# A graph kernel on one core: node rows moved as 112 and 13 partitions, the opening reordered, the second table by fifths in six banks

## The reference, cut to what matters

```
h = relu(layernorm(x)); x = x + L0(h)     # message layer: the part that the change touches most
   L0: m = relu(h[src] @ W_msg[:256] + h[dst] @ W_msg[256:] + b_msg)
       agg = segment_sum(m, dst); out = layernorm(relu([h, agg] @ W_upd + b_upd)) * gamma + beta
h = ...; x = x + L1(h)     # sums, maxima and means of edge attributes by node, then an MLP
h = ...; x = x + L2(h)     # attention over the edges
h = ...; x = x + L3(h)     # feat @ W_self + max over edges of (relu(feat @ W_pool))[src] * weight, @ W_neigh
```

## Time and profile before

| | |
|---|---|
| median of 3 runs | 2512.22 us (2509.89 to 2512.85) |
| profiled execution | 2510.97 us, span 2508.7 us |
| PE / DVE / ACT / GpSimd busy | 1118.0 / 1420.4 / 455.4 / 1437.0 us |
| share of the span | 45 / 57 / 18 / 57 % |
| DMA | 447.51 MB, mean 178 GB/s |

### The profile page before, as it was taken

One profiled execution on the slowest core, in us unless ns is written; L12 is line 12 of the kernel. 1 busy time (PEld: TensorE's weight loads), 2 busy tenths in 40 slices (PEclk: granted clock), 3 DMA queues, 4 the chain that ended last, 5 costly groups with the idle time before them and its releaser, 6 DMA issues. The chain is left out here.

```text
span 2508.7 us, 19387 instructions
## 1 busy us (share of the span) xinstructions
PE 1118.0 (45%) x4862; PEld 802.8 (32%) x4862; DVE 1420.4 (57%) x3644; ACT 455.4 (18%) x952; POOL 1437.0 (57%) x1447
## 2 busy tenths in 40 slices
PE   5597778787557249999930000000024111111105
PEld 4486667666334135556620000000013000000004
DVE  4397777676999932222236666666665444434342
ACT  3022222221011101111110000000014333333331
POOL 2577777776246040010057777777743777777774
PEclk9799999999766559999965555555557555555557
DMA  4697777775887720000036666666643666666663
GB/s 126 195 285 237 240 230 228 236 234 152 279 265 253 248 62 3 13 14 9 9 93 209 209 209 208 209 208 209 208 133 119 206 213 208 211 211 209 211 208 127
DMA packets 204961, 447.51 MB, mean 178 GB/s; under 512 B 38899, under 2 KB 114564, under 8 KB 204850
## 3 DMA queue, kind: packets, MB, share of 16 engines
q1 hardware_dynamic: 136107, 263.40, 29.4%
q0 software_dynamic: 67936, 182.02, 27.1%
q10 hardware_dynamic: 806, 0.87, 0.1%
HBM read 276.43 MB, written 169.68 MB: 178 GB/s over the span
## 5 line engine op out<-in xcount | busy, mean ns | idle before, releaser
L390 POOL DMA_INDIRECT msg_rows<-message_source_table,source x416 | 402.8, 968 | 193.7 <-issue 178.6
L1733 POOL DMA_INDIRECT att_rows<-att_table,lane_source x416 | 419.8, 1009 | 126.8 <-issue 126.8
L1754 POOL DMA_INDIRECT att_rows<-message_source_table,lane_source x416 | 393.5, 946 | 158.2 <-issue 126.4
L492 PE MATMUL msg_ps_sum<-msg_by_edge,msg_rows 128*128 128x128 f32 x1664 | 225.3, 293 | 97.7 <-DVE aggT L603 96.0
L492 PEld LDWEIGHTS msg_ps_sum<-msg_by_edge,msg_rows 128*128 128x128 f32 x1664 | 210.9, 204 | 129.3 <-issue 128.3
L1837 PE MATMUL late_ps<-ident,att_largest 128*4 128x128 f32 x1 | 0.4, 374 | 551.6 <-DVE att_largest L1963 551.6
L1885 PE MATMUL late_ps<-w_selfT,hT 128*125 128x256 f32 x100 | 49.7, 649 | 403.6 <-DVE x L2122 403.6
L480 PE MATMUL msg_ps_window<-msg_window,msg_by_node 128*128 128x256 f32 x832 | 206.4, 394 | 21.3 <-issue 21.3
L1309 POOL DMA_INDIRECT att_terms<-aggT,first_edge x25 | 29.5, 1180 | 323.9 <-ACT aggT L1433 323.9
L2115 DVE SCALAR_TENSOR_TENSOR att_rows<-att_rows,lane_line,late_ps_share 128x256 f32<-128x256 f32 x208 | 99.9, 480 | 173.8 <-ACT late_ps_share L1817 164.6
L1985 DVE SCALAR_TENSOR_TENSOR aggT<-aggT,lane_carry,att_rows 128x260 f32<-128x260 f32 x388 | 190.3, 490 | 13.6
(11 more groups left out here) (320 smaller groups left out, 2265.5 us busy)
## 6 DMA issues: line engine op xcount, KB each, us to landing
att_states<-aggT SPq DMA_DIRECT2D x104, 528.0 KB
msg_window<-message_window_table SPq DMA_DIRECT2D x416, 128.0 KB
best_states<-att_rows SPq DMA_DIRECT2D x104, 512.0 KB
attr_states<-attr_work SPq DMA_DIRECT2D x26, 768.0 KB
attr_states<-aggT SPq DMA_DIRECT2D x26, 768.0 KB
attr_work<-in_edge_attr SPq DMA_DIRECT2D x36, 384.0 KB
msg_line<-place_line SPq DMA_DIRECT2D x52, 256.0 KB
msg_rows<-message_source_table,source POOLq DMA_INDIRECT x416, 3.7
```

The costliest lines, as they stand in the source:

```text
L390: nc.gpsimd.indirect_dma_start(rows[:, s, t, :], None, self.source_table, bass.IndirectOffsetOnAxis(ap=self.source[:, at:at + 1], axis=0)) ...
L492: last = nc.tensor.matmul(ps_sum[s % 2][:, t, k, :], rows[:, s, t, k * P:(k + 1) * P], by_edge[:, s % BUFS, t, :], start=True, stop=True)
L1733: nc.gpsimd.indirect_dma_start(rows[:, t % ring, :], None, self.attention_table, bass.IndirectOffsetOnAxis(ap=self.lane_source[:, t:t + 1] ...
L1754: nc.gpsimd.indirect_dma_start(best_rows[:, g % SLOTS, t, :], None, self.source_table, bass.IndirectOffsetOnAxis(ap=self.lane_source[:, g ...
```

## The change

Six things change, the arithmetic of the outputs stays the same but for the broadcast of places by PE.

1. Every load or store of 125 partitions on SP's queue becomes two, of 112 and 13 partitions (`SHARES`): `x`, both tables, the attention table, the last source table and the output.
2. DVE makes the first fifth's statistics first; those of the next fifth come in two pieces behind the copies of the first and second block of a fifth, the aggregation behind the second, the reciprocal behind the fourth. ACT goes block by block, rows two blocks ahead of the copy. PE waits for the weights only before the first product.
3. The lists of first nodes are loaded from ACT's queue, behind all copies; the window loads wait for them.
4. Source stores are counted by fifths. The bias is added to a fifth as soon as that fifth's source rows are out. The products of the second table have six banks instead of two.
5. The places are no longer stored and spread by the DMA. PE spreads them (`spread_places`): a column of the identity in bf16, repeated 128 times, times `rel16`, into the first bank of the group's own `ps_window`; DVE compares from there. `rel16` stays in SBUF.
6. In the loop, PE's order becomes `gather_sums` 1, `spread_places` 5, `expand` 4; the wait for `added` moves from `expand` to `spread_places`. On DVE `add` and `by_nodes` change places.

```diff
+EVEN = NT // 16 * 16
+SHARES = (slice(0, EVEN), slice(EVEN, NT))
...
-            ps_table = [banks_window[0][0:NT, k * BANK:k * BANK + D] for k in range(2)]
+            ps_table = [ps[0:NT, k * BANK:k * BANK + D] for ps in (banks_window[0], *banks_sum) for k in range(2)]
...
                     for c, of in enumerate(parts):
-                        sp.dma_start(self.x[:, of.start:of.stop, :], a["x"][of.start * NT:of.stop * NT, :].rearrange(
-                            "(b p) d -> p b d", p=NT)).then_inc(x_in[c], 16)
-                    for tile, flat in first_nodes:
-                        sp.dma_start(tile, flat, allow_slow_non_contiguous=True).then_inc(lines_out, 16)
+                        rows_of_x = a["x"][of.start * NT:of.stop * NT, :].rearrange("(b p) d -> p b d", p=NT)
+                        for share in SHARES:
+                            sp.dma_start(self.x[share, of.start:of.stop, :], rows_of_x[share, :, :]
+                                         ).then_inc(x_in[c], 16)
                     for b in range(NB):
-                        if b == edges_at:
-                            sp.wait_ge(chain, lines_made)
-                            sp.dma_start(self.place_line.rearrange("(q r c) -> r q c", r=RT, c=P), rel16
-                                         ).then_inc(lines_out, 16)
                         sp.wait_ge(copied, b + 1)
-                        sp.dma_start(self.source_table[b * NT:(b + 1) * NT, :], by_source[:, b, :]
-                                     ).then_inc(sources_out, 16)
+                        self.store_block(sp, self.source_table, b, by_source[:, b, :], fifth_out[b // PART])
...
                     pool.wait_ge(edges_kept, 1)
-                    pool.wait_ge(sources_out, 16 * NB)
+                    for stored in fifth_out:
+                        pool.wait_ge(stored, 32 * PART)
...
+                    root_of(0)
+                    relu_rows(0)
+                    relu_rows(1)
+                    for b in range(NB):
+                        if b % PART == 2 and b + PART < NB:
+                            root_of(b // PART + 1)
+                        if b + 2 < NB:
+                            relu_rows(b + 2)
+                        act.wait_ge(tabled, b + 1)
+                        nc.scalar.copy(by_source[:, b, :], ps_source[b % 2][:]).then_inc(copied, 1)
+                    for tile, flat in first_nodes:
+                        act.dma_start(tile, flat, allow_slow_non_contiguous=True).then_inc(lines_out, 16)
...
                     def window_rows(b):
-                        if b >= 2:
-                            pe.wait_ge(biased, b - 1)
+                        if b == 2:
+                            pe.wait_ge(copied, NB)
+                        if b >= len(ps_table):
+                            pe.wait_ge(biased, b + 1 - len(ps_table))
...
+                    def spread_places(i, s):
+
+                        pe.wait_ge(ev["added"], self.freed(i, s, 2))
+                        for t in range(TG):
+                            q, r = divmod((i * SLOTS + s) * TG + t, RT)
+                            last = nc.tensor.matmul(
+                                banks_window[s % 2][:, t * P:(t + 1) * P], ident16[:, r:r + 1].to_broadcast([RT, P]),
+                                rel16[:, q, :], start=True, stop=True)
+                        last.then_inc(ev["spread"], 1)
+
                     def expand(i, s):
 
                         pe.wait_ge(ev["nodes_hot"], self.ready(i, s))
                         pe.wait_ge(*self.landed(self.window_in, i, s, TG))
-                        pe.wait_ge(ev["added"], self.freed(i, s, 2))
...
-                    pipelined(pe, [(gather_sums, 1), (expand, 4)])
+                    pe.wait_ge(biased, NB)
+                    pe.wait_ge(edges_kept, 3)
+                    pipelined(pe, [(gather_sums, 1), (spread_places, 5), (expand, 4)])
...
                     def turned_rows(b):
-                        if b % PART == 0 and b + PART < NB:
-                            scales(b // PART + 1)
                         dve.wait_ge(turned, b + 1)
                         nc.vector.tensor_copy(self.hT[:, :, b * NT:(b + 1) * NT], ps_turned[b % 2][:, :, 0:NT]
                                               ).then_inc(kept, 1)
+                        c, at = b // PART + 1, b % PART
+                        if c < len(parts):
+                            if at == 0:
+                                stats_of(parts[c][0:3])
+                            if at == 1:
+                                stats_of(parts[c][3:PART])
+                                variances(c)
+                            if at == 3:
+                                scales(c)
...
-                            dve.wait_ge(sources_out, 16 * NB)
-                            nc.vector.tensor_tensor(by_window[:, b, :], ps_table[b % 2][:], bias[:], ALU.add
+                            dve.wait_ge(fifth_out[b // PART], 32 * PART)
+                            nc.vector.tensor_tensor(by_window[:, b, :], ps_table[b % len(ps_table)][:], bias[:], ALU.add
...
-                        dve.wait_ge(*self.landed(self.line_in, i, s, groups=PAIR))
-                        nc.vector.tensor_scalar(by_node[:, s % BUFS, :], line[:, s % BUFS, :],
+                        dve.wait_ge(ev["spread"], self.ready(i, s))
+                        nc.vector.tensor_scalar(by_node[:, s % BUFS, :], banks_window[s % 2][:, 0:GE],
                                                 self.partition[:, 0:1], None, ALU.is_equal).then_inc(ev["nodes_hot"], 1)
...
-                    pipelined(dve, [(acc[0], 0), (by_nodes, 5), (acc[1], 0), (hot[0], 4), (hot[1], 4), (acc[2], 0),
-                                    (add, 3), (acc[3], 0)])
+                    pipelined(dve, [(acc[0], 0), (add, 3), (acc[1], 0), (hot[0], 4), (hot[1], 4), (acc[2], 0),
+                                    (by_nodes, 5), (acc[3], 0)])
...
+    def store_block(self, engine, table, b, rows, stored):
+
+        for share in SHARES:
+            engine.dma_start(table[b * NT + share.start:b * NT + share.stop, :], rows[share, :]).then_inc(stored, 16)
```

More of the change, by code:

```diff
@@ L244, in message_pass @@
             "loads", "clears", "marks", "when_made", "spread_made"))
[L245 to L249 removed]
+        w_loads, tabled, copied, windowed, biased, windows_out, tail_out, blank = (self.sem(f"msg_{k}") for k in (
+            "loads", "tabled", "copied", "windowed", "biased", "windows_out", "tail_out", "blank"))
+        x_in, fifth_out = self.index_in + self.line_in[0:1], self.window_in + self.line_in[1:2]
+        self.before.update((sem.name, 32) for sem in x_in)
+        self.before.update((sem.name, 32 * PART) for sem in fifth_out)
         steps_made, root, rstd, made, turned, kept = self.norm_events
@@ L1289, in _ @@
                         sp.wait_ge(termed, b + 1)
-                        sp.dma_start(self.attention_table[b * NT:(b + 1) * NT, :], out[:, b % ring, :]
-                                     ).then_inc(stores[b % ring], 16)
+                        self.store_block(sp, self.attention_table, b, out[:, b % ring, :], stores[b % ring])
                     for r in range(ring):
-                        sp.wait_ge(*self.past(stores[r], 16 * len(range(r, NB, ring))))
+                        sp.wait_ge(*self.past(stores[r], 32 * len(range(r, NB, ring))))
                     sp.wait_ge(listed, 16 * len(lists))
@@ L1552, in mlp @@
         for r in range(ring):
-            for sem in (stores[r], termed_out[r]):
-                self.before[sem.name] += 16 * len(range(r, NB, ring))
+            self.before[stores[r].name] += 32 * len(range(r, NB, ring))
+            self.before[termed_out[r].name] += 16 * len(range(r, NB, ring))
     def attention_and_best(self):
```

94 lines of the change are left out of this document (38 added, 56 removed).

## The result

Four runs of each kernel, on the same chip in turn: before 2511.05 us median (2509.0 to 2512.85), changed 2467.77 us (2463.19 to 2474.08). The ratio of the changed kernel's time to that of before is 0.983, 95% interval 0.9806 to 0.9854: 43 us faster. The profiled execution of the changed kernel took 2463.19 us, span 2461.4, and is the fastest of its four; against the profiled execution of before it gains 47.3 us of span. The forecast was 2477, its range for 8 in 10 was 2461 to 2496.

The account below looks back on a forecast made before the run. GpSimd's gathers, 5.09 us per group of four, were taken to bound the loop; gains of 28.4 (opening), 4 (last source table) and 2.5 (output) made 35 us off 2510.97, so 2476, median 2477; 8-in-10 range 2461 to 2496.

Parts of the forecast that it names:

- Number of engines: Split transfers: largest number up to 16 dividing the rows; 125 gives 5 engines, 112 gives 16, 13 gives 13.
- rival (c): Transfers do not spread, or two issues cost SP 0.9 us and more: gain 20, 2492 us; chance 0.06.
- Second issue and landing: Block stores: two issues take SP 0.65 us (bounds 0.53 and 0.9); a store lands in 2.4 us, not 4.6.
- my two signs of being wrong: GpSimd waiting for sums again and again through the loop, or SP's issues becoming the pace of the blocks.
- Chain A: Opening, source table stored to 32 gathers issued: start 6, middle 4, landing 3.6 us gained; first gather 54.4, free at 94.4.
- Chain B: Opening, window table stored to first sum: last bias 71.7, first window load 75.5, first matmul 79.4, GpSimd freed 92.3 us.
- A decides: Start of loop: source-table chain's 94.4 us is later than window-table chain's 92.3, so GpSimd's 14.8 us stall goes.
- The loop: Groups of four gathers: GpSimd's 5.09 us stays the limit over PE's and DVE's 4.4, so it costs 0.
- (a): Loop slows as the engines' handshake passes 5.09 us; at 5.6 it costs 49 us, 2525 us; chance 0.09.
- (b): Milder loop slowdown, 5.15 to 5.4 us a group: 6 to 30 us lost, about 2495 us; chance 0.14.
- My chain of 4.6 us: Loop, per group through PE and DVE: last accumulation 2.1, spread 0.5, expansion 1.9, then next sums: 4.6 us.
- rival (d): Gathers shorten too, if the compare from SBUF holds GpSimd up: whole 10 us excess could go, 2467 us; chance 0.06.

Follow-up runs that it names:

- kernel 1: The kernel before with only the split of 125-partition loads and stores into 112 and 13; 2482.52 us, ratio 0.9895.
- kernel 2: The changed kernel with transfers in one piece of 125 partitions again, all other edits kept; 2504.54 us, ratio 0.998.
- kernel 9: The changed kernel with shares of 96 and 29 rows instead of 112 and 13; 2554.23 us in one execution.
- kernel 6: The changed kernel with the next fifth's statistics, aggregation and scales in one lump before the copy of a fifth's first block; 2477.77 us, ratio 0.9867.
- kernel 4: The changed kernel with GpSimd's clear of aggT cut into pieces of 256 columns, 26 in all; 2471.54 us, ratio 0.9856.
- kernel 12: The changed kernel with aggT cleared by ACT, DVE and GpSimd, weights and bias first on ACT's queue, four blocks copied before the edge lists; 2470.59 us, ratio 0.9836.
- kernel 11: The changed kernel with every matmul of the spread made five times; 2473.5 us in one execution.
- kernel 3: The changed kernel with places stored and spread by DMA again, compared from SBUF, loop order as before; 2469.86 us, ratio 0.9847.
- kernel 10: The changed kernel with every matmul of the spread made three times; 2473.1 us in one execution.
- kernel 8: The changed kernel with the 52 line transfers and the place_line store also made, into a tile nothing computes with; 2472.31 us, ratio 0.9847.
- kernel 5: The changed kernel with aggT cleared in 26 pieces, weights and bias first on ACT's queue, one block copied before the edge lists; 2466.99 us, ratio 0.9825.

## Why the prediction was right, point by point

**Number of engines: right.** Kernels 1, 2 and 9 bear it out from three sides: 125 rows on SP's queue are slow, 112 and 13 fast, 96 and 29 slower than 125. The profile does not count the engines of a transfer; the runs show the pace. That is the divisor rule of the Trainium skill (DMA: Bandwidth & Descriptors, section on why a DMA increments its semaphore by 16); the runs agree with it, and the 16 engines that it gives 96 rows did not save a share of 29. The first half of rival (c), transfers that do not spread, is out.

**Second issue and landing: half right.** The 50 window stores took SP 23.28 us, 0.93 us a block, not 0.65 and over the bound of 0.9; so SP, not PE's 0.86, paced the second table's stores, the variant that I had priced at 1 us. It is also the condition in the second half of rival (c), and one of my two signs of being wrong, SP's issues as the pace of the blocks: both came true here. What the rival made of it did not: first gather 52.87, not 61, and GpSimd freed at 95.12, not 103. The last bias was at 69.99 (71.7 forecast; 23 steps of 0.86 us from 51 are 70.8, so 0.9 us of that was my arithmetic), the issues of the last store ended only at 73.0, 3.0 us after the start of that bias, the first window was loaded at 76.90 (75.5). At the end of the kernel the last wait fell from 4.6 to 1.1 us, more than the 2.2 I had allowed for, and the last gap from the addition to the end from 5.3 us to 2.3.

**Chain A: right within 2 us, term by term.** Start: 23.44 to 16.91 is 6.5 us for 6. Middle: from first to last copy 35.41 before, 29.76 after, 5.7 for 4; kernel 6 shows that the order of the statistics, with ACT's root, carries 4.5 of it, and kernel 1, which has the old order and the split, takes 34.50, so 0.9 goes with the split. (The last ten copies before are nine steps, 9.84 us, so 1.09 us each is right.) Landing: from last copy to first gather 9.17 before, 6.20 after, 3.0 for 3.6. The reason that I gave for the start was only partly the right one. What ended it was not the lists or weights: DVE's addition of 125 x 5 elements stood for 6.44 us until GpSimd's clear of `aggT` had ended. Without that hold the edge lists are next (kernel 4: DVE's first cast waits for them until 13.95), and without both the second fifth of x (kernel 12), so taking one or two of the three away gave nothing.

**Chain B: the step that failed was "A decides".** I had B free GpSimd at 92.3 and A at 94.4. A was ready at 92.67 (95.12 less the wait of 2.45), B at 95.12, so B decides. B was 1.7 us early at the last bias, lost 3.1 from there to the first window load (6.9 us for 3.8) and 1.6 between that and the first matmul (5.46 us for 3.9); from there 12.76 us for 12.9, with the additions at 86.10, 89.60 and 93.10, each behind an expansion. The two errors, A early and B late, left the freed time at 95.12 for 94.4 and the gain at 27.7 us for 28.4: that they nearly cancel is luck.

**The loop: no cost, and 5 us of gain that I had given to a rival.** The compare takes 0.742 us, not 0.68; the spread 0.40, not 0.5; both are covered. Rivals (a) and (b) are out: GpSimd waits for sums once (2.45 us) and 0.4 us more in the whole loop. My chain of 4.6 us (its terms, 2.1, 0.5 and 1.9, add to 4.5), which already left 0.4 us of room, was too long, since 0.88 us more of PE's work in it costs the steady loop nothing (kernel 11). The gathers fell from 0.968 to 0.956 us on average over all 416, so the last one was 5 us earlier again. That is rival (d) at half of its size: in three kernels that compare from SBUF (before, 1, 3) gathers take 967 to 968 ns on average, in ten of the eleven that compare from PSUM 954 to 960 ns, in the eleventh (kernel 10) 965. Kernel 8 takes the traffic out as a cause.

The traces show where the excess over 945 ns lies. Two long gathers, one of before and one of the changed kernel, each with what DVE runs at its start:

```profile
300.91 0.48 DVE L580 TENSOR_SCALAR msg_by_node<-msg_line,partition 128x512 f32<-128x512 bf16 x1
301.02 1.18 POOL L390 DMA_INDIRECT msg_rows<-message_source_table,source  x1 [0.30 <-issue]
...
319.68 0.75 DVE L692 TENSOR_TENSOR msg_by_edge<-columns,place 128x256 f32<-128x256 f32 x2
320.10 1.15 POOL L377 DMA_INDIRECT msg_rows<-message_source_table,source  x1 [0.31 <-issue]
```

Summed over the gathers from 125 to 570 us (kernel 9: from 175), by what DVE ran when the gather began:

| kernel | excess, us | at `by_edges` | at the place compare | else |
|---|---|---|---|---|
| before | 8.4 | 4.7 | 2.9 | 0.8 |
| 1 | 8.4 | 4.7 | 3.2 | 0.5 |
| 3 | 7.7 | 5.2 | 1.9 | 0.6 |
| changed | 4.2 | 4.1 | 0.0 | 0.1 |
| 8 | 3.3 | 3.1 | 0.0 | 0.2 |
| 10 | 7.1 | 6.3 | 0.2 | 0.7 |

The compare's own share, 1.9 to 3.2 us when it reads SBUF, is at most 0.2 in all eleven kernels where it reads PSUM. What is left lies with `by_edges`, both of whose inputs are in SBUF: in these eleven kernels all 323 gathers of over 1.0 us began while one ran. Its share moves between 3.1 and 6.3 us with no edit to `by_edges`, so, as I read it, how often the two meet depends on the timing of the loop; it is also where nearly all of kernel 10's larger excess lies. In every kernel here the order of `add` and `by_nodes` on DVE changes together with the compare's source, so the runs do not separate the two for this part. The rule of the Trainium skill (SBUF — State Buffer, "SBUF: two separate sides") fits the sign of the compare's share; that it is the shared port is the page's account, and the runs show only that this share goes when the compare reads PSUM.

**Late layers.** From the last attention gather to the last layer's first it is 95.6 us before and 92.2 after, 3.4 us for 4. The output gained the 3.0 us above (2.5).

**The sum.** 27.7 + 5 + 3.4 + 3 = 39 us, and 2510.97 less 39 is 2472, between the forecast of 2477 and what the runs gave, 2467.8; the 4 us that are left lie within the spread of the runs (2463 to 2474) and have no cause that is shown. Forecast and measurement differ mainly by the gathers.

## What to carry to other kernels

Look at the divisors of the outermost size of each transfer before its bytes: one odd partition count had slowed the loads of x, the stores of the tables and the output, and one badly chosen share (29) cost more than the whole fault. When several causes hold the same start, removing one can show little: 27 and 5 us apart were 43 together, and three fixes to the opening's start gave nothing, because another wait stood close behind. Before fearing for a handshake, add work to it in steps; here 0.88 us a group were free in the steady loop and cost 4 us at its start.

## What the runs showed of the hardware that was not expected

- A DVE addition of 125 x 5 elements takes 0.17 us alone and up to 6.85 us (kernel 8) when it meets GpSimd's clear of SBUF. In nine kernels it started between 7.99 and 13.63 us, and in each it ended at 14.83 to 14.86, with GpSimd's clear ending at 14.81 to 14.83. In eight of the nine it started 0.4 to 1.0 us ahead of GpSimd's first clear (8.96 to 8.99), while GpSimd issued DMAs, and was held all the same; at 7.87 (kernel 4) it went through in 0.19. Statistics and aggregation of DVE ran through in the same time (kernel 2, 11.51 to 13.60). Clearing in 26 pieces held it to the end of the last piece just the same (kernel 5).
- A gather of 128 rows takes 0.945 us, and up to 1.2 when DVE is comparing two SBUF tiles (`by_edges`) as it begins: so for all 323 gathers over 1.0 us in the loops of the eleven kernels that compare places from PSUM.
- Repeating a bf16 matmul of 104 rows and 128 columns costs 0.055 us each time (kernels 10 and 11), where one of f32 with 128 columns costs 0.25 (eight, which the profile counts as 16, in 2.02 us).
- With the spread matmuls in the loop the granted clock from 90 to 560 us is 1.00, that is 2.4 GHz throughout; in kernels 1 and 3, without them, it is 0.96. From 175 to 560 us, behind the start of the loop in every kernel, it is 0.99 to 1.00 in the eleven kernels with them and 0.95 to 0.96 in the three without, where PE is busy less of the time (0.81 before, 0.85 changed, 130 to 560 us).
- An issue on SP's queue takes 0.26 us in the output's stores before and 0.40 (median) in the window stores by 112 and 13; in the loads of x the longest takes 11.2 us before (125 rows), 5.4 by 112 and 13 and 11.3 by 96 and 29. Everything on that queue waits with it.
